# A decoder layer in split fp32: the second half of the cross-attention's output product as plain fp32 matmuls

## The reference

```python
x = _layernorm(x + _L0_attn_ref(x, ...))              # linear attention, 16 heads of 16
x = _layernorm(x + _L0_xattn_ref(x, ctx_1024, ...))   # softmax attention over 64 context rows, 16 heads of 64
x = _layernorm(x + _L0_ffn_ref(x, ...))               # 8 experts with a capacity
```

```python
q = x @ Wq.T; k, v = split(context @ Wkv.T)           # per head
attn = softmax(q k^T * 64 ** -0.5)
out = (attn v, heads side by side) @ Wout.T + b_out
```

## Time and profile before

| | us |
|---|---|
| median of 3 runs (1379.72 to 1382.04) | 1379.74 |
| the profiled execution, its own time | 1378.68 |
| its span, from the first to the last instruction | 1376.9 |
| TensorE busy (share of the span) | 1267.8 (92%) |
| VectorE busy | 897.4 (65%) |
| POOL busy | 607.0 (44%) |
| ScalarE busy | 530.6 (39%) |
| setup, attention phase, its drain, experts (roughly) | 0 to 136, 136 to 900, 900 to 990, 990 to 1377 |

### The profile page before, as it was taken

One profiled execution on the slowest core, in us unless ns is written; L12 is line 12 of the kernel. 1 busy time (PEld: TensorE's weight loads), 2 busy tenths in 40 slices (PEclk: granted clock), 3 DMA queues, 4 the chain that ended last, 5 costly groups with the idle time before them and its releaser, 6 DMA issues. The chain is left out here.

```text
span 1376.9 us, 24341 instructions
## 1 busy us (share of the span) xinstructions
PE 1267.8 (92%) x8016; PEld 1121.1 (81%) x8016; DVE 897.4 (65%) x1770; ACT 530.6 (39%) x1025; POOL 607.0 (44%) x962
## 2 busy tenths in 40 slices
PE   6966999999999999999999999888599999999997
PEld 5755888888888788888888888787479988999897
DVE  5534888888788788788788888787443233223333
ACT  2013354454444444544454544444351233213321
POOL 2104556566466466565565665554241221122201
PEclk9988999999999999999999999999889999999999
DMA  8641011111010111111111111310111110111000
GB/s 272 141 100 32 24 40 39 32 47 47 24 54 32 38 38 46 33 44 31 47 38 31 50 35 40 115 31 24 32 62 62 62 58 4 61 61 61 0 0 31
DMA packets 117427, 69.45 MB, mean 50 GB/s; under 512 B 74082, under 2 KB 114787, under 8 KB 117348
## 3 DMA queue, kind: packets, MB, share of 16 engines
q1 hardware_dynamic: 114228, 66.82, 16.5%
q10 hardware_dynamic: 3120, 1.71, 0.5%
HBM read 42.29 MB, written 26.22 MB: 50 GB/s over the span
## 5 line engine op out<-in xcount | busy, mean ns | idle before, releaser
L1365 POOL TENSOR_TENSOR w_lo<-w_raw,w_hi 128x2048 fp32r<-128x2048 f32 x16 | 73.7, 4608 | 240.7 <-ACT w_hi L1316 192.0
L1338 ACT ACTIVATE hT_hi<-up 128x512 fp32r<-128x512 f32 x128 | 76.1, 597 | 236.1 <-PE up L134 236.1
L132 PE MATMUL ob<-b_hi,pT_hi 128*128 128x256 f32 x512 | 158.6, 310 | 7.3 <-DVE pT_lo L719 7.0
L794 POOL TENSOR_TENSOR prob<-prob,rz 128x512 f32<-128x512 f32 x128 | 130.9, 1044 | 67.9 <-DVE rz L681 67.9
L1527 DVE SCALAR_TENSOR_TENSOR hT_lo<-up,hT_hi 128x512 fp32r<-128x512 f32 x128 | 88.3, 692 | 96.6 <-ACT hT_hi L1338 96.6
L132 PE MATMUL dn<-w_hi,hT_hi 128*128 128x256 f32 x512 | 145.0, 283 | 0.8 <-DVE acc L1536 0.8
L134 PE MATMUL ob<-b_hi,pT_lo 128*128 128x256 f32 x512 | 145.0, 283 | 0.0
L133 PE MATMUL ob<-b_lo,pT_hi 128*128 128x256 f32 x512 | 144.9, 283 | 0.0
L133 PE MATMUL dn<-w_lo,hT_hi 128*128 128x256 f32 x512 | 144.9, 283 | 0.0
L134 PE MATMUL dn<-w_hi,hT_lo 128*128 128x256 f32 x512 | 144.9, 283 | 0.0
L585 ACT ACTIVATE prob<-prob 128x512 f32<-128x512 f32 x128 | 80.6, 630 | 135.0 <-DVE prob L712 135.0
(11 more groups left out here) (207 smaller groups left out, 3504.7 us busy)
## 6 DMA issues: line engine op xcount, KB each, us to landing
xraw<-in_x SPq DMA_DIRECT2D x16, 512.0 KB, 3.9
kv_scratch<-stage SPq DMA_DIRECT2D x32, 256.0 KB, 2.6
x_scratch<-x SPq DMA_DIRECT2D x64, 128.0 KB, 1.7
out_x<-o_sb SPq DMA_DIRECT2D x64, 128.0 KB, 1.8
w_raw<-in_L_ffn_experts_inter SPq DMA_DIRECT2D x8, 1024.0 KB, 4.9
w_raw<-in_L_ffn_experts_out SPq DMA_DIRECT2D x8, 1024.0 KB, 7.4
kraw<-kv_scratch SPq DMA_DIRECT2D x32, 128.0 KB, 2.9
vraw<-kv_scratch SPq DMA_DIRECT2D x32, 128.0 KB, 2.9
```

Source lines behind the costliest of these rows:

```text
L132: pe.matmul(out, lh, rh, start=first, stop=False)
L794: pool.tensor_tensor(part, part, rz[:, q, h * 8:h * 8 + 8].unsqueeze(2).broadcast_to([P, 8, NKV]), ALU.mult).then_inc(s["p_ready"], 1)
L1338: act.activation(hT_hi[:, h, i, :], up[i % 4][:, :], ACT.Relu).then_inc(s["up_hi"], 1)
L1365: pool.tensor_tensor(lo[:, u, :, :], raw[:, :, :], f32(hi[:, u, :, :]), ALU.subtract).then_inc(s["w_lo_made"], 1)
```

## The change

The product of pairs 4 to 7 (h = 1) uses plain fp32 operands, one matmul for each pair. Its transposed probabilities are copied whole by ScalarE into `pT_whole`; this copy frees the bank, and VectorE's second pT_lo (L719 with h = 1) is gone. B2 and B3, the weights of those pairs, are copied whole by ScalarE into `b_whole` and have left `SPLIT` for `COPIED`. In slot 0 the second half waits for B2 (the later of the two in `ORDER`). The buffers of hi and lo are half as long.

```diff
-    COPIED = ("G", "GT", "R")
-    SPLIT = ("A0", "A1", "A2", "A3", "B0", "B1", "B2", "B3", "SW", "SB", "Q0", "Q1")
+    COPIED = ("G", "GT", "R", "B2", "B3")
+    SPLIT = ("A0", "A1", "A2", "A3", "B0", "B1", "SW", "SB", "Q0", "Q1")
@@ pe_pB
-            prep_done(pe, it, "B1" if h == 0 else "B3")
+            prep_done(pe, it, "B1" if h == 0 else "B2")
         for r in range(PAIRS // 2):
-            pr = h * (PAIRS // 2) + r
-            last = three_passes(pe, ob[:, 0:C], (pT_hi[:, pr, :], pT_lo[:, pr, :]),
-                                (b_hi[:, pr, :], b_lo[:, pr, :]), pr == 0, pr == PAIRS - 1)
+            if h == 0:
+                last = three_passes(pe, ob[:, 0:C], (pT_hi[:, r, :], pT_lo[:, r, :]),
+                                    (b_hi[:, r, :], b_lo[:, r, :]), r == 0, False)
+            else:
+                last = pe.matmul(ob[:, 0:C], pT_whole[:, r, :], b_whole[:, r, :], start=False, stop=r == PAIRS // 2 - 1)
@@ prep_views
+        if i >= 2:
+            return pw[:, :].rearrange("p (r c) -> p r c", r=2), b_whole[:, 2 * i - 4:2 * i - 2, :], None
@@ act_pT
-        act.activation(pT_hi[:, h * 4:h * 4 + 4, :], pt[:, :].rearrange("p (r u) -> p r u", u=P),
-                       ACT.Copy).then_inc(s["pt_hi_made"], 1)
+        src = pt[:, :].rearrange("p (r u) -> p r u", u=P)
+        if h == 0:
+            act.activation(pT_hi[:, :, :], src, ACT.Copy).then_inc(s["pt_hi_made"], 1)
+        else:
+            act.activation(pT_whole[:, :, :], src, ACT.Copy).then_inc(s["pt_taken"], 1)
@@ dve_slot
-            dve_pT(dve, n - 1, 0)
+            dve_pT(dve, n - 1)
...
-        if has_prev:
-            dve_pT(dve, n - 1, 1)
@@ buffers
-    b_hi = k.sb("b_hi", [P, PAIRS, C], F32R)
-    b_lo = k.sb("b_lo", [P, PAIRS, C], F32R)
+    b_hi = k.sb("b_hi", [P, PAIRS // 2, C], F32R)
+    b_lo = k.sb("b_lo", [P, PAIRS // 2, C], F32R)
+    b_whole = k.sb("b_whole", [P, PAIRS // 2, C])
...
-    pT_hi = k.sb("pT_hi", [P, PAIRS, P], F32R)
-    pT_lo = k.sb("pT_lo", [P, PAIRS, P], F32R)
+    pT_hi = k.sb("pT_hi", [P, PAIRS // 2, P], F32R)
+    pT_lo = k.sb("pT_lo", [P, PAIRS // 2, P], F32R)
+    pT_whole = k.sb("pT_whole", [P, PAIRS // 2, P])
```

More of the change, by code:

```diff
@@ L714, in dve_shift, with dve_pT @@
                           ALU.subtract).then_inc(s["sim_taken"], 1)
[L716 to L720, removed]
+    def dve_pT(dve, n):
+        need(dve, "pt_hi_made", n + 1)
+        dve.tensor_tensor(pT_lo[:, :, :], pt[:, :].rearrange("p (r u) -> p r u", u=P),
+                          f32(pT_hi[:, :, :]), ALU.subtract).then_inc(s["pt_taken"], 1)
     def pool_rstd(pool, ln, n, q):
```

## The result

Predicted were 1380.3 us, with 1374 to 1387 as the range. Measured: the changed kernel 1383.74 us (median of 20 runs, 1381.42 to 1387.34), the kernel before 1381.05 us (20 runs, 1379.55 to 1384.15). The ratio is 1.0026, with a 95% interval of 1.0018 to 1.0034: a little slower, on the edge of the 0.2% at which the prediction drew its line. The time is inside the range; the likeliest case, a change that can't be told, was missed narrowly. Of the 3.4 us between forecast and median, 1.3 are in the starting point: the three runs of before that were shown had a median of 1379.7, twenty have 1381.05. The other 2.1 us are what the experiments have to find.

What follows compares the result with a forecast made beforehand. TensorE was taken as close to its limit in the steady part. Steady +7.1 us (+17.6, -7.0, -3.2) and drain -6.5 gave +0.6, added to the shown runs' median 1379.7: 1380.3 us, range 1374 to 1387.

Steps and rivals of the forecast that it cites:

- the likeliest case: Whole kernel: gains and cost level within 0.2%, 1380.3 us, no change that can be told; chance 0.48.
- The longer product: TensorE's second half-product: plain 1.74 us against split 1.42, +0.32 us per tile, 64 tiles, 20.5 us if nothing hides it.
- only passes count: Rival: a split matmul is worth one of four passes, so the change costs 0.43 a tile; 1387 us, chance 0.05.
- Q0's wait: Slot 3, first Q product: xT_lo starts 0.54 us earlier once the subtraction goes, 13 times, -7.0 us.
- The absorption at x: Slot 3: TensorE's L392 waits for ScalarE's x, hiding 0.32 us of slot 2's longer product in 10 sequences, -3.2 us.
- The drain: Last two sequences: second halves no longer wait for VectorE's subtraction, -6.5 us, bounds -3 and -8.
- the part that the clock was to give: Drain, half-product at 958.82: without the 2.18 us idle before it, full clock instead of half; 3.6 us with its wait.
- the sum's last: Steady part +7.1 and drain -6.5 give +0.6 us on the profiled execution, added to the shown runs' median 1379.7.
- nothing absorbed: Rival: x in slot 3 waits for the moved A1 copy; 3.2 us lost, 1383.5 us, up to 1388; chance 0.22.
- VectorE's relief reaching farther: Rival: sums and reciprocal before xT_lo start earlier, Q0's wait goes whole; up to 8 us more, 1372 us; chance 0.25.

Runs made afterwards that it cites:

- the relief alone: Changed kernel with the second half as 12 split matmuls again, all reading ScalarE's copies, low parts left out; 1367.87 us, 0.9910 of the kernel before.
- the written-out form: Sequence loop written out so nothing jumps: changed kernel 1368.86 us, ratio 0.9916; kernel before 1369.60 us, 0.9923; both ratios against the looped kernel before.
- the price alone: Changed kernel with VectorE's second subtraction put back, into a spare buffer, with its old wait; 1393.47 us, ratio 1.0088 to the kernel before.
- the kernel that has nothing else: Kernel before with the plain second half only in the last eight tiles (sequences 14 and 15); 1374.41 us, ratio 0.9964.

## Why the prediction came out as it did

**The longer product**: right. Predicted 0.32 a tile, measured 0.30 to 0.31, from the rows of SW, a product of another stage with the same shape. The rival in which only passes count would have needed 0.43, and does not hold. The Trainium skill ("FP8 and Floating Point Precision", section TensorE Precision Notes) gives true FP32 four passes. The trace agrees, in that a plain matmul costs 0.435 us, four times 0.109; but the three split ones it replaces cost 0.12 each.

**Q0's wait**: right in its place and cause, and too high in its size: -0.54 in 13 sequences was the forecast. Where slot 3 starts on an early record, 0.19 is to be taken off its length (17.71 before, 17.31 and 17.67 after in turn), so it changed by -0.59 in one looped sequence and by -0.23 in the next, as the wait before Q0 did (1.10 to 0.51 and to 0.88); the slot's own longer product and what is absorbed at x cancel. The mean is -0.41. The issue gap of 0.23 before xT_lo was not foreseen; the relief alone shows that it comes with the subtraction's going, the written-out form that it needs the loop.

**The absorption at x**: right, the most doubtful step with a margin of 0.06 us. It stands in both one-sided experiments: the wait gone with the price alone, whole with the relief alone.

**The drain**: -6.5 forecast, -6.3 measured in the profiled pair, -6.1 in the kernel that has nothing else. Inside it, the part that the clock was to give (1.6 of the 6.5) held less firmly than the sum, and in the pair it came out by luck. A stretch of half clock stood behind the wait of 2.18 us in the first execution of the kernel before and behind another wait in the second. Of the four executions of the changed kernel two have one, behind a wait of 1.50 us that the relief does not touch, and those drains are 99.7 and 99.8 us instead of 98.2. On average over all six executions (104.5 and 103.7 us before; 98.2, 98.2, 99.7 and 99.8 after) the drain gained 5.1 us and not 6.3.

**The step that failed** is the sum's last: "+0.6 us on the profiled execution", carried to the median as it stood. It took the earlier trace rows, full clock from 136 to 900, as a property of the kernel. It is one of an execution, and the row could not have shown otherwise. A stretch of 3.4 us at half clock lowers a mean over 764 us by 0.002, which the two decimals hide: the same window still reads 1.00 in the changed kernel's execution with two such stretches in it. The kernel before has 6.8 us of half clock in it too. They begin within its wait of 4.2 us for the mask, which ended at 892.73:

```profile
890.80:897.60 6.80, 4.87 (x12) 3.85 (x13) 1.56 (x3) 0.49 (x1) 1.38 (x4) 0.50 0.28 36
```

Behind the 1.8 to 2.1 us waits at the jumps, which the earlier trace rows hold as the long ones of their second row, the clock can fall as well. I read the 12.4 us as unchanged, which they are, and asked no further.

**How far this is shown.** All four stretches seen inside the loop, in any version, stand right behind a jump's wait. None is seen with the jumps written out, nor with both halves plain. By the averages above, these stretches and those of the drain have the size of what is missing. The mean granted clock of the timed runs can't be used to count them. In the changed kernel's 20 timed runs it is 0.979 to 0.981 in nine, with times of 1381.6 to 1383.6 us, and 0.975 or 0.976 in seven, with 1386.0 to 1387.3; one stretch lowers it by 0.0012. But it also holds the set-up. The first execution has 0.977 with no stretch in loop or drain, since its set-up was at a lower clock than before's (0.88 and 0.91, the figure ahead of the DMA share):

```profile
0.00:138.33 138.33, 105.90 (x476) 84.35 (x477) 66.30 (x127) 25.14 (x49) 32.79 (x64) 0.88 0.52 135
0.00:136.04 136.04, 102.39 (x477) 82.04 (x478) 65.22 (x127) 24.93 (x49) 32.73 (x64) 0.91 0.53 138
```

And the kernel before had 0.976 in three of its 41 runs beside the experiments, two of them with no more than 1381.3 and 1381.6 us. By time alone, the 4 to 5 us between the two groups would be about three stretches.

**What stays open**: why the changed kernel falls into them more often than the kernel before, whose waits there are as long (1.80 to 2.08 us in both). Over all looped executions with these waits, the clock fell behind 4 of 20 where the second half is plain throughout (the changed kernel four times, and the price alone) and behind none of 16 where it is split (the kernel before twice, its version with the plain half in the drain alone, and the relief alone). That points at the longer product and not at VectorE's relief, but it is too few to prove it. Two sequences take the changed kernel 109.9 us from one jump's wait to the next, and the kernel before 108.9 to 109.2; whether that distance matters was not tried. No execution above 1386 us was profiled, nor one of the kernel before above 1380, whose median of 20 is itself 2.4 us above its profiled execution. So what the kernel before has in its longer executions is not known either.

The rivals: nothing absorbed is out; only passes count is out; VectorE's relief reaching farther is out in the loop, where its gain was smaller than forecast. The change came out slower by a cause that none of the three named. That the time still lies well inside the range is in part luck: the range was made for other causes.

## What to carry to other kernels

A price taken start to start from the same shape elsewhere in the trace was good to 0.01 us, and a single record at a change of kind would have misled by 0.19. Before trading one engine's work against another's, look at the long waits at the loop's jump: here four waits worth some 8 us stood behind VectorE's late start. Moving one half (this change) left them whole; with both halves moved, or the loop written out, they were gone. And where plain products relieve an engine, use them in the stage in which TensorE waits. With the loop written out, both halves plain gave 7 us in the drain alone (1362.8 against 1369.6 us) and nothing in the whole kernel (1370.3). Last, a forecast from one profiled execution holds for that execution: the clock in another one can differ, and a window of hundreds of us does not show it.

## What the runs showed of the hardware

- VectorE's first instruction behind the loop's jump came 2.45 to 2.72 us late with nothing but "issue" in front, at all four jumps of all six executions of the two kernels (before 350.57, again 352.78). With both halves plain, where a pass has 160 counted VectorE instructions instead of 172 or 184, it came some 0.1 us late. With the loop written out the delay is gone, and pT's waits fell from 12.4 to 5.0 us.
- Inside the looped body one more gap of 0.23 us stands before the same VectorE instruction in every other sequence, and not in the written-out program.
- A wait of 1.5 to 2.2 us of a TensorE that is busy on both sides is followed by 3.4 us at half clock in some executions and not in others, at the same instruction. Each such stretch cost 1.4 to 1.6 us. At the wait of 4.0 to 6.0 us for the mask the clock fell in every execution, for 3.4 or 6.8 us, at some point between 2.7 us before the end of the wait and 1.2 us behind it.
- A plain fp32 matmul of 256 columns cost 0.435 us and a split one 0.118, start to start at full clock. The first split matmul behind a plain one was recorded 0.19 us early.
